# Rows of two layer norms turned by transposing DMAs, and a second Square on ScalarE

## What is computed

```python
h = jnp.take(embed_table, input_ids, axis=0)              # (64, 256, 256), nan_to_num
h = h + attn(_layernorm(h), Wf, Wi, Wh)
h = h + ffn(_layernorm(h), fast_b, w_fc, w_proj, u, v, gate)

# attn: sigmoid(x Wf) and sigmoid(x Wi) gate a scan over time of g(x Wh), in log space
# ffn:
h = _bitlinear(x, w_fc) + gate * (x @ v.T @ fast_b.T @ u.T)
r = jnp.maximum(h, 0.0)
return _bitlinear(r * r, w_proj)
```

## Time and profile before

| | |
|---|---|
| time, median of 3 runs | 1036.16 us (1035.92 to 1037.06) |
| span of the profiled execution | 1033.3 us |
| TensorE busy | 968.8 us, 94% |
| VectorE busy | 864.6 us, 84% |
| ScalarE busy | 553.0 us, 54% |
| GpSimd busy | 489.6 us, 47% |
| the page's DMA queues | 7.7% of sixteen engines' time |

### The profile page before, as it was taken

The page is one execution under the profiler, slowest core; times in us unless marked ns, Lnnn a source line. Parts: engine busy times, 40 slices in busy tenths (PEclk is TensorE's granted clock), DMA queues, the critical chain, the costliest instruction groups (busy, mean ns, idle before and its releaser), DMA issues.

```text
span 1033.3 us, 18090 instructions
## 1 busy us (share of the span) xinstructions
PE 968.8 (94%) x5825; PEld 582.6 (56%) x5825; DVE 864.6 (84%) x1570; ACT 553.0 (54%) x775; POOL 489.6 (47%) x427
## 2 busy tenths in 40 slices
PE   1779999999999999999999999999999999999987
PEld 1336655556655555665556566555656655566654
DVE  6897888888888888888888888888898888888673
ACT  3355566545556644555664455566445556545543
POOL 6525455445545544554554454555445455442210
PEclk9899999999999999999999999999999999999998
DMA  4000000000000000000000000000000000000001
GB/s 128 10 1 8 25 26 25 21 25 25 5 26 25 24 22 25 25 5 26 25 23 23 25 25 5 26 25 23 23 26 26 5 25 25 21 25 22 21 1 41
DMA packets 26582, 24.30 MB, mean 24 GB/s; under 512 B 5190, under 2 KB 25232, under 8 KB 26560
## 3 DMA queue, kind: packets, MB, share of 16 engines
q1 hardware_dynamic: 20416, 19.81, 5.8%
q0 software_dynamic: 6144, 4.21, 1.8%
HBM read 19.81 MB, written 16.78 MB: 35 GB/s over the span
## 4 chain that ended last, share of the span: by engine, by line
PE 44%; DVE 30%; issue 14%; POOL 6%; ACT 3%; DVEq 1%; DMA 1%; POOLq 1%; SPq 0%; ACTq 0%
PE y_ps L659 20%; PE bank L576 16%; DVE normed L741 6%; DVE hid L921 6%; DVE sq_hi L961 4%; POOL value L323 4%; DVE x_lo L747 3%; PE turned L645 3%; PE turned L493 3%; DVE cand L912 2%; DVE rows_pos L719 2%; ACT cand_lin L413 2%; DVE low L937 2%; DVE rows_neg L721 1%; POOL rstd L295 1%
## 5 line engine op out<-in xcount | busy, mean ns | idle before, releaser
L659 PE MATMUL y_ps<-proj_t,sq_hi 128*128 128x256 bf16 x1024 | 225.3, 273 | 0.0
L659 PE MATMUL y_ps<-proj_t,sq_lo 128*128 128x256 bf16 x1024 | 225.3, 273 | 0.0
L283 POOL DMA_INDIRECT rows_raw<-table,idx_now x128 | 184.8, 1444 | 58.3 <-issue 30.2
L623 PE MATMUL bank<-x_hi,fc_t 128*128 128x512 f16 x512 | 195.8, 382 | 0.7 <-issue 0.7
L625 PE MATMUL bank<-x_lo,fc_t 128*128 128x512 f16 x512 | 195.5, 382 | 0.0
L413 ACT ACTIVATE forget<-bank,w_back 128x512 f32<-128x512 f32 x64 | 44.0, 687 | 278.3 <-PE bank L576 278.3
L444 ACT ACTIVATE relu<-bank,relu_scale 128x512 f32<-128x512 f32 x256 | 164.5, 681 | 16.8 <-PE bank L629 16.8
L323 POOL TENSOR_TENSOR value<-inp,cand 128x512 f32<-128x512 f32 x64 | 81.9, 1279 | 187.2 <-DVE cand L912 187.2
L963 DVE TENSOR_TENSOR sq_lo<-sq,sq_hi 128x1024 f16<-128x1024 f32 x128 | 156.9, 1225 | 4.4
L741 DVE TENSOR_SCALAR normed<-h,moments,rstd 128x256 f32<-128x256 f32 x256 | 119.5, 529 | 43.5 <-POOL rstd L295 43.5
L576 PE MATMUL bank<-x_hi,w_hi 128*128 128x512 f16 x384 | 147.0, 383 | 2.4 <-issue 2.4
(11 more groups left out here) (140 smaller groups left out, 1348.1 us busy)
## 6 DMA issues: line engine op xcount, KB each, us to landing
out<-out_sb SPq DMA_DIRECT2D x32, 512.0 KB, 3.0
rows_raw<-table,idx_now POOLq DMA_INDIRECT x128, 3.0
fc_raw<-w_fc SPq DMA_DIRECT2D x1, 1024.0 KB, 7.0
pj_raw<-w_proj SPq DMA_DIRECT2D x1, 1024.0 KB, 9.1
w_raw<-wf SPq DMA_DIRECT2D x1, 256.0 KB, 3.2
w_raw<-wi SPq DMA_DIRECT2D x1, 256.0 KB, 3.5
w_raw<-wh SPq DMA_DIRECT2D x1, 256.0 KB, 4.1
ids_sb<-ids SPq DMA_DIRECT2D x1, 64.0 KB, 1.8
```

Of the source, the lines that this page charges most:

```text
L283: pool.indirect_dma_start(rows_raw[:, par, j, :], None, table, bass.IndirectOffsetOnAxis(ap=idx_now[:, par, j:j + 1], axis=0), bounds_chec ...
L623: pe.matmul(dst[:, :], fc_t[:, k, f * P:(f + 1) * P], x_hi[1][:, k, :], start=(k == 0), stop=False)
L659: ins = pe.matmul(y_ps[:, j, :], part[:, f, j * P:(j + 1) * P], proj_t[:, f, :], start=(f == 0 and j % 2 == 0 and part is sq_hi), stop=(f ...
```

## The change

The rows of both norms are split before they are turned. `x_high` (ScalarE) converts `normed` to the f16 rows of `x_rows`, and `x_low` (VectorE) writes the rest beside them. SP then turns each half by one transposing DMA (128 x 1024 f16, 256 KB) into `x_cols`, four of them in a step, and TensorE waits for `x_landed` and reads x_cols. The sixteen transposes of normed rows on TensorE go; those of hid move from behind f = 7 to behind f = 5; `low_rank` moves from behind gate group 3 to behind 4. `x_cols` of the first norm has two buffers, that of the second has one, so its DMAs wait until the step's f matmuls are done.

`sq_hi` is no longer a copy of sq on VectorE: ScalarE squares relu a second time, with f16 output. The guard on VectorE becomes one bounding pass (rows_fin) and one scalar_tensor_tensor in place of two passes and a sum.

The core of the diff:

```diff
+            def turn_rows(k, c, par):
+
+                for part, ready in enumerate((x_hi_ready[k], x_lo_ready[k])):
+                    sp.wait_ge(ready, c + 1)
+                    pass_on(sp, sp_passed, c)
+                    sp.dma_start_transpose(x_part(k, par, part).rearrange("p j k t -> p (j k) t"),
+                                           x_rows[k][:, part, :, :].rearrange("p j d -> p (j d)"))\
+                        .then_inc(x_landed[k], 16)
...
             def step(n, h, par):
+                if known_below(n, N - 1):
+                    wait(sp, gate_done, 6 * n)
+                    pass_on(sp, sp_passed, n)
+                    turn_rows(0, n + 1, 1 - par)
+                if known_below(n, N):
+                    wait(sp, fc_done, FC * n)
+                    pass_on(sp, sp_passed, n)
+                    turn_rows(1, n, 0)
...
             def x_high(k, c):
 
-                act.wait_ge(x_turned[k], c + 1)
-                act.activation(x_hi[k][:, :, :], turned_cols, ACT.Copy).then_inc(x_hi_ready[k], 1)
+                act.wait_ge(normed_ready[k], TILES * (c + 1))
+                wait(act, x_landed[k], 32 * c)
+                act.activation(x_rows[k][:, 0, :, :], normed[k][:, :, :], ACT.Copy).then_inc(x_hi_ready[k], 1)
...
                         act.activation(sq[:, p % 2, :, :], relu[:, p % 2, :, :], ACT.Square)\
                             .then_inc(sq_ready, 1)
-                    if p == 1 and known_below(n, N - 1):
-                        act.wait_ge(gate_done, 6 * (n + 1))
-                        x_high(0, n + 1)
+                        wait(act, y_done, m)
+                        act.activation(sq_hi[:, 2 * p:2 * p + 2, :], relu[:, p % 2, :, :], ACT.Square)\
+                            .then_inc(sq_hi_ready, 1)
...
+                if front:
+                    x_high(1, n)
...
             def low_rank(n, m, front):
-                pe.wait_ge(x_hi_ready[1], m + 1)
-                pe.wait_ge(x_lo_ready[1], m + 1)
+                pe.wait_ge(x_landed[1], 32 * (m + 1))
...
-                dve.tensor_tensor(x_lo[k][:, :, :], turned_cols, x_hi[k][:, :, :], ALU.subtract)\
+                dve.tensor_tensor(x_rows[k][:, 1, :, :], normed[k][:, :, :], x_rows[k][:, 0, :, :], ALU.subtract)\
                     .then_inc(x_lo_ready[k], 1)
...
-                        dve.tensor_copy(sq_hi[:, 2 * p:2 * p + 2, :], sq[:, p % 2, :, :]).then_inc(sq_hi_ready, 1)
...
                 if front:
                     normalise(1, n, h1[:, par, :, :])
+                if front:
+                    x_low(1, n)
```

More of the change, by code:

```diff
@@ L424, in step @@
                                     .then_inc(a_summed, 1)
-                            if back and (e, q) == (1, 0):
+                            if (e, q) == (1, 0) and known_below(n, N - 1) and not (isinstance(n, int) and n == 1):
+                                x_high(0, n + 1)
+                            if back and (e, q) == (1, 1):
                                 low_high(m)
@@ L549, in low_rank @@
                 for k in range(KD):
-                    pe.matmul(bank[0][:, :], low_a[:, k, :], x_hi[1][:, k, :], start=(k == 0), stop=False)
-                    ins = pe.matmul(bank[0][:, :], low_a[:, k, :], x_lo[1][:, k, :], start=False, stop=(k == KD - 1))
+                    for part in range(2):
+                        ins = pe.matmul(bank[0][:, :], low_a[:, k, :], x_part(1, 0, part)[:, :, k, :],
+                                        start=(k == 0 and part == 0), stop=(k == KD - 1 and part == 1))
                 ins.then_inc(low_done, 1)
@@ L574, in step @@
                             for w in (w_hi, w_lo):
[L575 to L578, removed]
+                                for part in range(2):
+                                    ins = pe.matmul(bank[gate_bank[p]][:, :], w[:, k, q, :],
+                                                    x_part(0, par, part)[:, :, k, :],
+                                                    start=(k == 0 and w is w_hi and part == 0),
+                                                    stop=(k == KD - 1 and w is w_lo and part == 1))
                         ins.then_inc(gate_done, 1)
[L580 to L583, removed]
+                        if back and p == 4:
                             low_rank(n, m, True)
@@ L622, in step @@
                         for k in range(KD):
[L623 to L626, removed]
+                            for part in range(2):
+                                pe.matmul(dst[:, :], fc_t[:, k, f * P:(f + 1) * P], x_part(1, 0, part)[:, :, k, :],
+                                          start=(k == 0 and part == 0), stop=False)
                         if f == 0:
@@ L630, in step @@
                             .then_inc(fc_done, 1)
[L631 to L634, removed]
                     if isinstance(n, int) and n == 1 and f in (1, 2, 4, 5):
                         turn_proj((1, 2, 4, 5).index(f))
[L637 to L647, removed]
+                    if front and f == 5:
+                        pe.wait_ge(scanned, 4 * (n + 1))
+                        wait(pe, h1_ready, n)
+                        for j in range(TILES):
+                            for e in range(KD):
+                                ins = pe.transpose(turned_rows[:, j, e * P:(e + 1) * P],
+                                                   hid[:, e, j * P:(j + 1) * P], ident[:, :])
+                        ins.then_inc(hid_turned, 1)
                 if back:
@@ L933, in step @@
                     scan(0)
+                if known_below(n, N - 1) and not (isinstance(n, int) and n <= 1):
+                    x_low(0, n + 1)
                 if back:
```

71 lines of the change are left out of this document (24 added, 47 removed).

## The result

The changed kernel takes 1235.84 us (median of 4 runs, 1234.05 to 1236.67) against 1036.32 us before: the ratio is 1.193, 95% interval 1.191 to 1.195. It is slower by 199.5 us. The forecast was 1215 us with a range of 1130 to 1330.

A forecast was written before the change was run, and what follows sets the result against it. TensorE bounds before; after, a chain through the other engines takes 34.95 us per step against 30.33. Span 1033.3 + 138 (30 x 4.6) + 30 (clock) + 10 (ends) = 1211, in round numbers 1215 us; range 1130 to 1330.

The forecast's parts named there:

- (a): From low ready, through low_u of f = 0 and five matmuls of f = 1, to ScalarE: 1.66 us without the clock.
- (b): ScalarE's row of relu, relu, sq, sq_hi, from the relu of f = 1 to the last sq_hi's end: 12.37 us.
- (c): sq_lo of the last pair, h1, statistics and moments on VectorE: 4.37 us.
- (e): normed, x_high, x_low and y_sb of the second norm, one after another: 4.84 us.
- (f): From y_sb's end through out_sb to the end of the first norm's root: 3.85 us, + 0.03.
- (g): normed of the first norm on VectorE, beside GpSimd's value: 2.41 us, against 1.38 without value.
- (h): scan to low, x_low of the first norm, then low, on VectorE: 3.06 us.
- The clock: TensorE at half speed behind its new waits: between 0 and 2.4 us per step, taken as 1.0.
- The landing: A transposing DMA's landing: 4 us, bounds 2 and 9.1; free within 6.9 us of the second norm's low part.
- The slow DMA: Rival: transposing DMAs land in 9.1 to 12 us, past their cover, giving 1281 to 1368 us; chance 0.20.
- That TensorE stays the bound: Rival: the chain is shorter than TensorE's 27.9 us per step and its waits vanish, giving 973 us; chance 0.04.
- The third: Rival: normed and value don't collide and the clock holds, chain 33.5 to 33.9 us, 1141 us; 1040 to 1130 chance 0.07.

The follow-up runs named there:

- late_dma: The changed kernel with the low half of the second norm's rows turned twice, so low_rank gets its columns about 3 us later: 1250.49 us, ratio 1.208.
- the fastest kernel: The kernel before with only the first norm's rows turned by transposing DMAs, and with the changed guard: 999.91 us, ratio 0.967.

## Why the prediction was right

The direction, the cause and most of the size held. Point by point, once round the chain, forecast against the rows above:

| | forecast | measured |
|---|---|---|
| (a) low to relu of f = 1, with 1.0 for the clock | 2.66 | 2.84 (558.38 to 561.22) |
| (b) relu, sq, sq_hi | 12.37 | 12.29 (to 573.51) |
| (c) sq_lo, h1, statistics | 4.37 | 4.58 (to 578.09) |
| (d) root of the second norm | 2.36 | 2.37 (to 580.46) |
| (e) normed, x_high, x_low, y_sb | 4.84 | 4.86 (to 585.32) |
| (f) out_sb, root of the first norm | 3.88 | 4.48 (to 589.80) |
| (g) normed beside value | 2.41 | 2.16 (to 591.96) |
| (h) scan, x_low, low | 3.06 | 3.15 (to 595.11) |
| sum | 35.95 | 36.73 |

0.78 us per step, 23 us in all, is the gap from 1215 to 1236. It is a net figure: six terms came out 1.11 us longer together, (b) and (g) 0.33 shorter. Its largest term is (f), which was mis-sized: from out_sb's end to rstd's it took 1.76 us (587.84 to 589.60), before 1.32 (555.42 to 556.74). The forecast took over a stretch in which VectorE did statistics and the second norm's x_lo; now cand runs beside out_sb and the small instruction of the root (0.67 us in place of 0.23), and takes 1.27 us itself where it takes 0.69 at 559.02. The rest of (f) is 0.2 us from rstd to normed in place of 0.03. (c) is 0.2 us longer: sq_lo starts 0.13 us behind sq_hi's end where 0.03 was taken, and h1 1.26 us behind sq_lo where it was 1.15.

**The clock** was put at 1.0 us of 0 to 2.4. (a) without it was forecast at 1.66 and came at 1.55 when TensorE was kept busy; with it 2.84. So it costs 1.3 us there, which is the first of the two amounts; the second, 1.1 us at f = 3, did not come: (b) is no longer than forecast, the clock being back at 561.1 us. That a value taken between the two, 1.0, is near 1.3 is partly luck. The run with repeated matmuls gave back 31 us; its turns take 35.5 us, where the forecast without the clock's part was 34.95.

**The landing** was taken as 4 us between 2 and 9.1; it is 3.2. It was free, as argued, as long as TensorE's clock is up (late_dma). A nearer row than the store's was on the page of the kernel before, a load of the same 256 KB:

```profile
w_raw<-wf SPq DMA_DIRECT2D x1, 256.0 KB, 3.2
```

The rule of the Trainium skill that transposing DMAs are as fast as regular ones (Advanced Engine Details and Errata, X-Bar Transpose (TRN2)) is borne out in the landing: 3.2 us for 256 KB either way. SP's own time for one is another matter: 1.24 us, against 0.37 for a store. The Trainium skill's 1309 ns for one block (VectorE: DVE Perf Modes, The three transpose paths) doesn't add up over the eight blocks of one DMA: the estimate of 10.5 us stands against 3.2.

**Rivals.** The slow DMA fell by 3.2 us and by late_dma. That TensorE stays the bound fell by its 80%; the run with more work on TensorE was faster. The third fell by (g), 2.16 us beside value where it is 1.38 alone, and by the clock. The trace also has what the prediction said it would show: forget 4.2 us behind its gate, sq_hi 0.95 us behind sq. What the prediction did not say: that the second Square is the costliest of the parts that were run singly (74 us alone, 67 us undone), and that the gain was there to be had by turning the first norm only.

## What to carry to other kernels

When one engine is busy for 94%, close the chain through the others once before taking work off it: here 1.7 us less on TensorE met a chain grown to 36.7 us, and the one piece of work that was added, the second Square, went to an engine that was idle for 46% on average. Take work off the bound engine where there is slack behind it (in the fastest kernel SP has issued the first norm's DMAs at 545.69, and the gates start to read the columns at 558.81), not where the result is the next thing waited for, and look at what an instruction stands behind in every queue, the idle ones too: one store's place on SP was worth 64 to 67 us.

## What the runs showed of the hardware

In the changed kernel a transposing DMA of 128 x 1024 f16 lands 3.2 us after its issue (median of 128; 3.0 to 4.9), and SP is occupied for 1.24 us by each (median), where the store of 512 KB takes it 0.37 us. The page's packets rose from 26582 to 161750 for these 128 DMAs, 1056 each, all of them under 512 B, some 250 bytes on average. None of this had a row in the trace of before. Waits of 1.4 us in each step left the mean granted clock at 0.986 (the second Square alone). In the changed kernel it fell to half for 3.4 us around the wait of 4 us (0.936 in all), and with that gap partly filled by repeated matmuls the mean stayed at 0.989.
